# Gathered rows turned by copies between partition groups and 32x32 blocks on VectorE, in place of TensorE transposes, in the expert loop of a gated cross-attention block

## The reference

```python
x = x + jnp.tanh(g_xattn[0]) * attention(_layernorm(x), ctx_1024, Wq, Wkv)
xn = _layernorm(x)
logits = jnp.einsum('bsd,de->bse', xn, gate_w) + gate_b
probs = jax.nn.softmax(logits, axis=1)
vals, idx = jax.lax.top_k(probs, 2)
h = jax.nn.relu(jnp.einsum('bsd,edo->ebso', xn, w1) + b1[:, None, None, :])
h = jax.nn.relu(jnp.einsum('ebso,eop->ebsp', h, w2) + b2[:, None, None, :])
y = jax.nn.relu(jnp.einsum('ebso,eop->ebsp', h, w3) + b3[:, None, None, :])
v = jnp.einsum('ebso,bse->eo', y, w_tok)     # w_tok: vals at the two chosen experts, else 0
out = jnp.einsum('bse,eo->bso', ind, v)      # ind: 1 at the two chosen experts, else 0
x = x + jnp.tanh(g_ffn[0]) * out
```

## Time and profile before

| what | value |
|---|---|
| median of 3 runs | 970.67 us (970.24 to 970.91) |
| profiled execution, its own time | 970.13 us |
| its span, first to last instruction | 968.4 us |
| mean granted PE clock | 0.984 |
| PE busy | 940.8 us (97%) |
| DVE, ACT, POOL busy | 658.6, 419.3, 443.7 us |
| DMA | 49619 packets, 109.82 MB |

### The profile page before, as it was taken

The page is one execution under the profiler, slowest core; times in us unless marked ns, Lnnn a source line. Parts: engine busy times, 40 slices in busy tenths (PEclk is TensorE's granted clock), DMA queues, the critical chain, the costliest instruction groups (busy, mean ns, idle before and its releaser), DMA issues.

```text
span 968.4 us, 19175 instructions
## 1 busy us (share of the span) xinstructions
PE 940.8 (97%) x6018; PEld 891.8 (92%) x6018; DVE 658.6 (68%) x1430; ACT 419.3 (43%) x634; POOL 443.7 (46%) x402
## 2 busy tenths in 40 slices
PE   9999999999999979999999999999999999999985
PEld 6999898998988869999999999999999999999981
DVE  5668788887888867866666666666666666666646
ACT  5454444534443454444444444444444444444311
POOL 4224544445343477564444444444444444444213
PEclk9999999999999989999999999999999999999995
DMA  6432322323211532442424555521321331331008
GB/s 229 153 131 94 126 87 87 125 95 127 87 65 68 177 105 64 133 133 89 132 88 132 175 175 175 174 90 45 128 93 45 125 96 45 121 100 47 16 16 347
DMA packets 49619, 109.82 MB, mean 113 GB/s; under 512 B 26032, under 2 KB 26288, under 8 KB 44848
## 3 DMA queue, kind: packets, MB, share of 16 engines
q1 hardware_dynamic: 42160, 92.01, 28.3%
q0 software_dynamic: 7424, 17.38, 5.9%
HBM read 92.25 MB, written 17.11 MB: 113 GB/s over the span
## 4 chain that ended last, share of the span: by engine, by line
PE 91%; DVE 6%; issue 1%; ACT 1%; POOL 1%; DMA 0%; DVEq 0%; POOLq 0%; ACTq 0%
PE bank L1256 27%; PE bank L1257 27%; PE bank L1258 27%; PE bank L1484 3%; DVE x_all L1246 2%; PE bank L1270 1%; PE bank L1326 1%; PE bank L1367 1%; PE bank L1369 1%; DVE x_all L974 0%; DVE st L869 0%; PE bank L1318 0%; PE bank L1316 0%; PE bank L1290 0%; DMA wq_raw<-in_wq_t 0%
## 5 line engine op out<-in xcount | busy, mean ns | idle before, releaser
L628 POOL TENSOR_TENSOR h_lo<-h,h_hi 128x704 fp32r<-128x704 f32 x96 | 170.9, 1781 | 279.4 <-DVE h_hi L1137 279.3
L1256 PE MATMUL bank<-h_hi,w_hi 128*128 128x352 f32 x752 | 246.5, 328 | 2.0 <-DVE base L921 1.1
L1258 PE MATMUL bank<-h_hi,w_lo 128*128 128x352 f32 x752 | 242.8, 323 | 0.0
L1257 PE MATMUL bank<-h_lo,w_hi 128*128 128x352 f32 x752 | 242.0, 322 | 0.0
L877 DVE TENSOR_TENSOR w_lo<-w_raw,w_hi 128x2048 fp32r<-128x2048 f32 x72 | 181.9, 2527 | 57.5 <-ACT w_hi L779 53.5
L779 ACT ACTIVATE w_hi<-w_raw 128x2048 fp32r<-128x2048 f32 x72 | 137.8, 1916 | 115.5 <-PE bank L1258 115.5
L790 ACT ACTIVATE h<-bank,bias 128x352 f32<-128x352 f32 x192 | 96.0, 552 | 205.5 <-PE bank L1258 196.8
L1137 DVE CAST h_hi<-h 128x704 fp32r<-128x704 f32 x96 | 51.6, 540 | 137.5 <-ACT h L790 135.6
L1256 PEld LDWEIGHTS bank<-h_hi,w_hi 128*128 128x128 f32 x752 | 142.1, 189 | 2.9 <-issue 2.8
L1257 PEld LDWEIGHTS bank<-h_lo,w_hi 128*128 128x128 f32 x752 | 142.0, 189 | 0.0
L1258 PEld LDWEIGHTS bank<-h_hi,w_lo 128*128 128x128 f32 x752 | 141.4, 188 | 0.0
(11 more groups left out here) (198 smaller groups left out, 1773.1 us busy)
## 6 DMA issues: line engine op xcount, KB each, us to landing
w_raw<-in_w SPq DMA_DIRECT2D x36, 1024.0 KB, 4.9
wb<-slot_pair SPq DMA_DIRECT2D x24, 352.0 KB, 3.5
xt_raw<-in_x_t SPq DMA_DIRECT2D x16, 512.0 KB, 4.0
c_raw<-in_ctx_t SPq DMA_DIRECT2D x16, 512.0 KB, 3.3
x_all<-in_x SPq DMA_DIRECT2D x16, 512.0 KB
xn_dram<-xn SPq DMA_DIRECT2D x16, 512.0 KB, 2.9
out<-x_all SPq DMA_DIRECT2D x16, 512.0 KB, 4.6
xg<-xn_dram,idx POOLq DMA_INDIRECT x72, 5.2
```

The source lines that it names most:

```text
L628: pool.tensor_tensor(h_lo[n][:, 2 * k:2 * k + 2], h[:, 2 * k:2 * k + 2], h_hi[n][:, 2 * k:2 * k + 2].bitcast(F32), ALU.subtract).then_inc( ...
L1256: pe.matmul(out_ap, lh, rh, start=(i == 0), stop=False)
L1257: pe.matmul(out_ap, lh, rl, start=False, stop=False)
L1258: last = pe.matmul(out_ap, ll, rh, start=False, stop=(i == n - 1))
```

## The change

For the tiles 4 and on, PE does no row transposes. Instead SP issues 16 DMAs for each tile (`quarters`). Quarter q of each gathered row is 128 features. The DMA (q, g) copies quarter q of the rows on the partitions 32g to 32g+31 of `xg` to the partitions 32q to 32q+31 of a new tensor `xq`, in runs of 512 bytes; there are 11 groups of 32 slots in a tile, and a DMA with g = 3 copies two of them, the others three. Then one DVE instruction (`transpose_blocks`) transposes the 44 blocks of 32x32 of `xq`, [128 x 1408] float32, into `et`. Within a quarter it reads the features i x 4 + k for i = 0 to 31, a step of 16 bytes. `et_high` and `et_low` become one instruction each, which read `et` in SBUF and not PSUM. Layer 1 thereby has feature 128q + 4i + k on partition 32q + i, chunk k. So `w1`'s rows are loaded in that order, by 4 DMAs of 32 partitions with runs of 2 KB in place of one DMA of 128 partitions. For the tiles 0 to 3 PE still transposes, and it reads the features dc, dc+4, dc+8, ... of `xg` in place of 128 neighbours.

`quarters(j + 2)` stands first in SP's `tile(j)`. It waits for the gather of tile j+2 and for `et_los` of tile j+1. `transpose_blocks(j + 2)` stands in DVE's order between `h_high(0, j + 1)` and `w_low(0, j + 2)`. `gather(m)` waits for the 16 copies of tile m-1 where it waited for PE's transposes. PE's wait in `layer2_half` stays as it is.

```diff
+QB = 32
+NQ = P // QB
+BY_BLOCKS = 4
...
+    W_IN = [16 * NQ, 16, 16]
...
+            xq = alloc(ph, "xq", [P, TILE // QB, P], F32)
+            et = alloc(ph, "et", [P, DC, TILE], F32)
...
                 def load():
-                    sp.dma_start(w_raw[n][:], w_dram[n][bass.ds(e, 1)].rearrange("a p c d -> (a p) c d")
-                                 ).then_inc(w_in[n], 16)
+                    if n > 0:
+                        sp.dma_start(w_raw[n][:], w_dram[n][bass.ds(e, 1)].rearrange("a p c d -> (a p) c d")
+                                     ).then_inc(w_in[n], 16)
+                    else:
+
+                        for q in range(NQ):
+                            rows = w_dram[0][bass.ds(e, 1), :, q].rearrange("a (i k) d -> i (a k) d", k=DC)
+                            sp.dma_start(w_raw[0][q * QB:(q + 1) * QB], rows).then_inc(w_in[0], 16)
...
+            def quarters(m):
+
+                need(sp, gathered, 16 * TH * (m + 1))
+                wait_alone(sp, "sp")
+                need(sp, et_los, TH * m)
+                wait_alone(sp, "sp")
+                for q in range(NQ):
+                    for g in range(NQ):
+                        n = (TILE - g * QB - 1) // P + 1
+                        sp.dma_start(xq[q * QB:(q + 1) * QB, g::NQ], xg[g * QB:(g + 1) * QB, 0:n, q * P:(q + 1) * P]
+                                     ).then_inc(xq_in, 16)
+
             def tile(j, left):
+                if has_tile(2, left) and not isinstance(j, int):
+                    quarters(j + 2)
...
-                need(pool, te_done, TH * m)
+                if isinstance(m, int) and m <= BY_BLOCKS:
+                    need(pool, te_done, TH * m)
+                else:
+                    need(pool, xq_in, 16 * NQ * NQ * (m - BY_BLOCKS))
...
+                if not isinstance(m, int):
+                    act.wait_ge(et_ready, m - BY_BLOCKS + 1)
+                    act.activation(et_hi[:], et[:], ACT.Copy).then_inc(et_his, TH)
+                    return
...
+            def transpose_blocks(m):
+                dve.wait_ge(xq_in, 16 * NQ * NQ * (m - BY_BLOCKS + 1))
+                need(dve, et_his, TH * m)
+                dve.transpose(et[:].rearrange("p k (g b) -> p g k b", b=QB),
+                              xq[:].rearrange("p g (i k) -> p g k i", k=DC)).then_inc(et_ready, 1)
+
             def et_low(m):
+                if not isinstance(m, int):
+                    dve.wait_ge(et_his, TH * (m + 1))
+                    dve.tensor_tensor(et_lo[:], et[:], et_hi[:].bitcast(F32), ALU.subtract).then_inc(et_los, TH)
+                    return
...
                 if has_tile(2, left):
+                    if not isinstance(j, int):
+                        transpose_blocks(j + 2)
                     w_low(0, j + 2)
                     et_low(j + 2)
...
-                        last = pe.transpose(row_banks(m)[c][:, dc * n:(dc + 1) * n], xg[0:n, c, dc * P:(dc + 1) * P],
+                        last = pe.transpose(row_banks(m)[c][:, dc * n:(dc + 1) * n], xg[0:n, c, dc::DC],
                                             ident[0:n, 0:n])
...
-                if has_tile(2, left):
+                if has_tile(2, left) and isinstance(j, int):
                     row_transposes(j + 2)
```

More of the change, by code:

```diff
@@ L335, in flamingo_block @@
         idx_in, wb_in, gathered = sem("idx_in"), sem("wb_in"), sem("gathered")
+        xq_in, et_ready = sem("xq_in"), sem("et_ready")
         te_done, et_his, et_los = sem("te_done"), sem("et_his"), sem("et_los")
@@ L453, in load_w @@
                 with sp.Else():
-                    sp.sem_inc(w_in[n], 16)
+                    sp.sem_inc(w_in[n], W_IN[n])
             def load_b(n, m):
@@ L776, in split_w @@
             def split_w(n, m):
-                act.wait_ge(w_in[n], 16 * (m + 1))
+                act.wait_ge(w_in[n], W_IN[n] * (m + 1))
                 need(act, l_done[n], 2 * m)
```

## The result

The kernel became slower: 1036.88 us, the median of 4 runs (1034.85 to 1037.36), against 970.79 us before (970.24 to 971.05). The ratio is 1.0675, 95% interval 1.0661 to 1.069. The forecast was 959, faster than before, with a range of 949 to 985; the change went the other way. The profiled execution took 1037.22 us with a span of 1035.4, which is 67.0 us more than before.

What follows compares the result with a forecast made beforehand. PE, busy 97%, bound the kernel at 24.27 us per tile; afterwards a loop through SP and DVE of 23.3 plus 0.4 gather wait gives 23.7, so 20 x (23.7 - 24.27) = -11.4: 959 us, range 949 to 985.

Steps and rivals of the forecast that it cites:

- T: DVE's block transpose of 1408 columns per tile: taken as 1.63 us, bounds 0.9 and 3.1.
- the prediction's loop: One turn per tile through SP's issues, the copies, DVE and weighted sum back to SP: 23.3 us, above PE's 23.07.
- idx to the first copy: On SP, three idx DMAs ahead of the next tile's copies: 1.40 us per tile.
- the 16th copy is issued 15 steps behind the first: SP's issues of the copies, 0.47 us apart with bounds 0.39 and 0.53: 7.1 us per tile.
- rival C: DVE's transpose takes about two cycles per element because of its 16-byte step: 975 to 988 us, likeliest 982; chance 0.32.
- SP's own work: SP's work per tile without waits: 13.9 us, plus 7.5 for sixteen issues and w1 loads, 22.1, below the period of 23.7.
- PE's wait ahead of layer 2: PE waits there for et_low; PE idle 0.3 to 0.9 us per tile expected.
- PE's wait of T - 2.1: PE's wait for et_low costs nothing up to T = 2.1 us, and T - 2.1 per tile above it.
- rival D: Copies land as late as a gather, 3.2 us, or the gather is held 1.1: 973 to 985 us; chance 0.10.
- the floor of 23.07: PE's three layers of 7.69 us: a tile without transposes can't be shorter than 23.07 us.
- The wait for the gather: SP's remaining wait ahead of idx, counted in the loop: 0.4 us per tile, between 0 and 1.7.
- PE's transposes of the tiles 0 to 3: PE's 48 transposes reading xg in 16-byte steps: taken as 0, 4.8 us if each took twice its 0.10.

Runs made afterwards that it cites:

- the two prices: Two kernels computing nothing of the reference, which time series of 8 DMA issues on SP and DVE reads by steps; copies inside SBUF came 0.63 to 0.69 us apart.
- the 2-copies kernel: The changed kernel with 2 DMAs moving the same bytes in place of 16, rows not regrouped by quarter: 965.55 us, ratio 0.9918 to before.
- the kernel with T put right: The changed kernel with the transpose reading 32 neighbouring features and w1's rows following, tiles 0 to 3 not adapted: 1016.11 us, ratio 1.0436 to before.
- the moves to ACT: ACT issues part of the 16 copies: 5 in the changed kernel, 988.95 us; with neighbours and w1 in one DMA, 5 give 959.89 and 9 give 950.1 us.
- the kernel before plus copies: The kernel before with the 16 copies per tile added on SP into a tensor nobody reads, PE still transposing: 982.34 us, ratio 1.009.
- nine on ACT: The changed kernel with the transpose reading neighbours, each w1 load one DMA, 9 copies issued by ACT and 7 by SP: 950.1 us, ratio 0.9757 to before.
- the fastest kernel: The same kernel as nine on ACT: 950.1 us, ratio 0.9757 to before.
- w1 in one DMA: The changed kernel with w1 laid out on the host so that each load is one DMA of 128 partitions: 1032.35 us, ratio 1.0596 to before.
- neighbours and w1 in one DMA: The changed kernel with the transpose over 32 neighbours and w1 in DRAM in both orders, one DMA per load: 1014.35 us, ratio 1.0427 to before.

## Why the prediction was wrong, point by point

One loop, term by term, in the tile from 680.14 to 707.38 us, each term from start to next start (so T is 2.62 where the instruction is listed with 2.70):

| term of the prediction's loop | predicted | measured |
|---|---|---|
| 1st to 16th issue of the copies | 7.1 | 9.70 |
| landing and hand-over to DVE | 1.9 | 1.97 |
| T, the block transpose | 1.63 | 2.62 |
| `w_low` | 2.29 | 2.17 |
| `et_low` | 1.64 | 1.54 |
| weighted sum to part_done | 3.58 | 3.67 |
| part_done to wb | 2.24 | 2.07 |
| wb to idx | 1.35 | 1.35 |
| idx to the first copy | 1.40 | 2.15 |
| hand-overs | 0.2 | in the others |
| sum | 23.3 | 27.24 |

- **The step that failed: "the 16th copy is issued 15 steps behind the first".** It was taken at 0.47, from loads out of DRAM, with bounds of 0.39 and 0.53. The measured step is 9.70/15 = 0.647, outside both. No row of before showed a DMA with both ends in SBUF, but the upper bound was also not the dearest issue of that trace. SP's timeline of the kernel before, a little behind the lines of the earlier trace rows, has loads of the same shape as those, 256 KB each:

```profile
3.58 0.65 SPq L391 DMA_DIRECT2D wq_raw<-in_wq_t  x1
4.27 0.61 SPq L392 DMA_DIRECT2D wk_raw<-in_wk_t  x1
```

These two start 0.69 apart. With 0.65 to 0.69 as the upper bound the same sum gives 26 us or more, and the forecast could not have rested on 0.47. Multiplied by 15 in a closed loop, 0.18 us are 2.6. By itself this puts the loop at 25.9, above 24.27, where the forecast had 0.94 us of room. Shown by the two prices, by the 2-copies kernel (the sign turns), by the kernel with T put right (it does not turn), and by the moves to ACT. It is the largest wrong term, but the sign does not hang on it alone: the measured loop with a step of 0.47 would be 27.24 - 2.6 = 24.6, still above 24.27, because of the next two points. No run has that step.
- **T.** The 1.63 was right for an instruction that reads neighbours (1.65) and wrong for this one, 2.7: rival C, though not at its two cycles per element (3.1), but at 1.6 times the pace of neighbours. The Trainium skill (Advanced Engine Details and Errata, Memory Cachelines) asks for two accesses in a line of 16 bytes; the transpose and the subtraction agree (1.65 and 1.64 at 2 elements, 2.65 both at 4), a copy with the same step does not (1.52). C had 0.32 of the chance and was true as a mechanism, but not as the cause: it alone would have given 24.3 per tile, about no change.
- **The gap behind idx.** From the first idx to the first copy it took 2.15, not 1.40: `quarters` has two waits with register arithmetic ahead of its first DMA, which the sum left out. 0.75 per tile, read off the timeline and not tested by itself.
- **SP's own work.** Put at 22.1 with a step of 0.47, the loads of `w1` in it (0.7). With 0.647 it is 24.2 without these loads, measured as 24.70 in the kernel before plus copies, and 27.74 in tiles with four loads of `w1`. So even without the loop, SP was full. (The 13.9 in it is the waits divided by 20; the window of the earlier trace rows is 19 periods long, which makes 13.4. It changes nothing here.)
- **The entry.** The sum was 20 periods. The one-time stall of 10.73 us in tile 4 was not in it: the copies of the first tile have nothing to hide behind, and `et_low` waits for all of them. 9.5 us, a seventh of the loss. It too hangs on the issues: the first transpose starts at 445.0 us with 16 copies on SP, at 436.9 with 2 and at 437.6 with nine on ACT.
- **Right:** PE's transposes are gone and worth 1.21 each; the loop through SP, the copies, DVE and `part` as the limit that takes PE's place, with six of its terms within 0.2 us; PE's wait ahead of layer 2; PE's wait of T - 2.1 where the loop is short (23.72 per tile with two copies); landing at 1.9 (rival D is out); the floor of 23.07; and the pace of a transpose of neighbours.
- **The wait for the gather,** put at 0.4 per tile, was 0: SP came to it so late that it was there in all but one tile. In the fastest kernel, where SP comes earlier, it is back with 17.3 us in 9 waits, and hides behind PE.
- **PE's transposes of the tiles 0 to 3** with the step went from 141 ns of weight load to 213 (median), and cost nothing that can be seen: the first block transpose starts at 443.1 us in the kernel with this step and one load of `w1` (w1 in one DMA), and at 443.0 in the one that also lacks the step (neighbours and w1 in one DMA).

In sum: 19 x (27.23 - 24.27) + 9.5 = 65.7 of the 67.0 us of span, and of the 3.9 us by which the loop is longer than predicted, the issue step is 2.6, T 1.0, the gap behind idx 0.75, and the other terms together -0.4.

## What to carry to other kernels

When work leaves the bounding engine and a queue gets many small DMAs for it, multiply the price of one issue by their number first, and take it from a DMA with the same two ends (here SBUF to SBUF); a price with one end in DRAM was 28% too low and was the largest error of the sum. Where no such row exists, bound it by the dearest issue in the whole trace, not by the nearest rows. Draw the loop that the new steps close, from issue to issue, and compare it with the old period; then spread the issues over two queues, which here turned +6.75% into -2.4%, and let the transposing engine read neighbours, and lay the weights out to fit.

## What the runs showed of the hardware that was not expected

- Issues of DMAs with both ends in SBUF are 0.63 to 0.69 us apart on SP, from 16 to 192 KB and for 32 or 128 partitions; with either end in DRAM and as many bytes 0.46 to 0.49. Pieces of 256 KB out of DRAM were 0.64 apart in one run, and in the kernel before first 0.47 and then 0.60 to 0.69. The four loads of `w1` took 0.58 each to issue with one order of rows in DRAM and 0.33 with another. The cause is open. On ACT's queue three of the copies in a row took 1.98 us, 0.66 each.
- A subtraction on DVE reads float32 at full pace up to a step of 2 elements, 1408 columns in 1.64 us; at 3 it takes 2.04, from 4 on 2.65 to 2.69. A copy with step 4 took 1.52, one of neighbours 1.62.
- A gap of PE costs more than itself. Busy time and granted clock (the column PEclk) of the kernel after, around the gap of 2.44 us:

```profile
694.00:698.30 4.30, 1.90 (x12) 1.61 (x10) 4.30 (x5) 2.30 (x2) 3.16 (x2) 0.97 0.90 354
698.30:700.00 1.70, 1.66 (x6) 1.66 (x7) 1.54 (x4) 1.00 (x1) 0.00 (x0) 0.50 0.38 109
700.00:702.00 2.00, 2.00 (x10) 2.00 (x10) 1.77 (x8) 0.00 (x0) 0.00 (x0) 0.63 0.00 0
702.00:704.00 2.00, 2.00 (x14) 2.00 (x13) 1.79 (x3) 0.07 (x1) 0.00 (x0) 1.00 0.04 1
```

Right behind the gap the granted clock is 0.50, the lower of its two levels, 1.2 GHz, and matmuls start 0.29 us apart where they were 0.16 (698.80, 699.09, 699.38 against 694.12, 694.29, 694.45); from 702 us on it is 1.00 again. Here it cost nothing that can be seen, since PE is not in the loop that sets the period of 27 us. In a kernel bound by PE such a gap would cost its 2.4 us and, as an estimate from these rows, some 1.6 us more (1.70 x 0.5 + 2.00 x 0.37); that was not run.
- ACT's sequencer issues DMAs while its compute part runs an activation (646.36 and 646.37 above).
